# Layer 0 of a two-layer gated cross-attention: value products in pairs, a turned row maximum with full-width weights, and another operation for its rounding

## The reference, cut to what matters

```python
energy = jnp.einsum('nqhd,nkhd->nhqk', q, k)
energy = jnp.where(mask == 0, jnp.float32(-1e+20), energy)
attn = jax.nn.softmax(energy * (1.0 / E ** 0.5), axis=3)
out = jnp.einsum('nhqk,nkhd->nqhd', attn, v).reshape(N, Sq, E)
```

## Time and profile before

| | |
|---|---|
| median of 3 runs | 1371.55 us (1370.35 to 1372.52) |
| the profiled execution | 1371.72 us |
| its span | 1370.0 us |
| PE busy | 1223.5 us, 89% of the span |
| DVE busy | 1026.2 us, 75% |
| ACT busy | 769.0 us, 56% |
| POOL busy | 395.0 us, 29% |
| mean granted TensorE clock | 0.972 |

### The profile page before, as it was taken

How to read it: one execution, slowest core, us unless ns; L and a number is a source line. 1 busy time by engine, 2 the same in 40 slices (tenths; PEclk the granted TensorE clock), 3 DMA queues, 4 the chain that set the end, 5 groups by cost and what they waited for, 6 DMA issues and landing times.

```text
span 1370.0 us, 27816 instructions
## 1 busy us (share of the span) xinstructions
PE 1223.5 (89%) x10408; PEld 760.9 (56%) x10408; DVE 1026.2 (75%) x1662; ACT 769.0 (56%) x1013; POOL 395.0 (29%) x248
## 2 busy tenths in 40 slices
PE   0869899999999996788799999999999999999974
PEld 0335565566566566334356666656666666666642
DVE  6656666666666646877888888888888888888877
ACT  0525455555555555455666666666666666666642
POOL 6357666666566415332000000000000000000000
PEclk9979999999999997999999999999999999999996
DMA  5223244234333420010011110011110011110000
GB/s 151 76 78 79 80 114 113 77 101 110 96 90 104 116 58 18 0 46 0 8 38 46 46 44 22 25 45 45 45 45 20 26 44 45 45 45 23 1 0 14
DMA packets 29717, 74.66 MB, mean 54 GB/s; under 512 B 6384, under 2 KB 14960, under 8 KB 29664
## 3 DMA queue, kind: packets, MB, share of 16 engines
q1 hardware_dynamic: 23408, 70.78, 17.7%
q10 hardware_dynamic: 6256, 3.16, 0.9%
HBM read 42.30 MB, written 0.46 MB: 31 GB/s over the span
## 4 chain that ended last, share of the span: by engine, by line
PE 69%; DVE 13%; issue 8%; ACT 7%; ACTq 3%; POOL 0%; DVEq 0%
PE bank L826 13%; PE bank L808 13%; PE bank L768 8%; PE bank L684 7%; PE bank L708 5%; PE bank L712 5%; PE bank L725 4%; DVE bank_max L1497 3%; ACTq L416 2%; DVE region L1639 2%; PE bank L849 2%; ACT region L1141 2%; PE bank L797 2%; DVE e_row L1458 2%; PE bank L1053 2%
## 5 line engine op out<-in xcount | busy, mean ns | idle before, releaser
L1458 DVE CUSTOM_DVE_ANT_0 e_row<-bank,region 112x1500 f32<-112x1500 f32 x128 | 220.1, 1720 | 129.4 <-PE bank L684 128.4
L1176 ACT CAST region<-bank 125x768 f16<-125x768 f32 x224 | 178.7, 798 | 206.2 <-PE bank L768 206.2
L1141 ACT ACTIVATE region<-bank 125x896 f32<-125x896 f32 x192 | 176.0, 917 | 210.0 <-PE bank L712 209.9
L808 PE MATMUL bank<-region 128*128 128x500 f16 x1008 | 234.6, 378 | 14.7 <-ACT e_row L1167 13.3
L1516 DVE TENSOR_TENSOR region<-bank,region 125x768 f16<-125x768 f32 x224 | 209.7, 954 | 25.4 <-ACT region L1176 25.4
L1497 DVE TENSOR_REDUCE bank_max<-bank 128x1 f32<-128x500 f32 x336 | 208.8, 671 | 10.6 <-PE bank L808 10.6
L514 POOL TENSOR_TENSOR region<-c_in,region 125x1536 f16<-125x1536 f32 x16 | 49.7, 3108 | 560.8 <-ACT region L1191 560.8
L768 PEld LDWEIGHTS bank<-ident,e_row 128*125 128x125 f32 x1344 | 175.5, 188 | 31.2 <-DVE region L1516 5.5
L768 PE MATMUL bank<-ident,e_row 128*125 128x128 f32 x1344 | 179.5, 273 | 3.3 <-DVE region L1516 2.6
L1167 ACT ACTIVATE e_row<-bank,neg_max 128x1500 f32<-128x1500 f32 x112 | 169.7, 1515 | 20.2 <-DVE neg_max L1501 20.0
L808 PEld LDWEIGHTS bank<-region 128*128 (+1 forms) x1008 | 93.3, 98 | 115.6 <-issue 11.4
(11 more groups left out here) (212 smaller groups left out, 1471.0 us busy)
## 6 DMA issues: line engine op xcount, KB each, us to landing
c_in<-in_ctx SPq DMA_DIRECT2D x32, 750.0 KB
region<-region SPq DMA_DIRECT2D x64, 192.0 KB, 2.7
region<-in_mask_Bx1xSxS_if SPq DMA_DIRECT2D x32, 328.1 KB
region<-region SPq DMA_DIRECT2D x64, 96.0 KB, 2.5
region<-region SPq DMA_DIRECT2D x8, 750.0 KB
g_w<-region SPq DMA_DIRECT2D x8, 750.0 KB
g_w<-in_L_ffn_rt_gate ACTq DMA_DIRECT2D x1, 1024.0 KB, 9.9
u_w<-in_L_ffn_rt_up ACTq DMA_DIRECT2D x1, 1024.0 KB, 17.4
```

Source lines behind the costliest of these rows:

```text
L808: last = pe.matmul(bank[:, k, 0:4 * KP], q1[:, ql, b, 128 * t:128 * (t + 1)], c_t1[par][:, cl, 4 * k:4 * k + 4, 0:KP], start=(ql == 0 and ...
L1141: act.activation(p0[:, 2 * i:2 * i + 2, :], ring0("s", h, i)[0:KP, :, 0:HALF_ROWS], ACT.Exp, scale=SCALE0)\
L1176: act.copy(p_high1[grp][:, UC * u:UC * (u + 1), 128 * at:128 * (at + 1)], pair_chunks(unit_no(1, par, ("turn", t, u)), 128)).then_inc(sem( ...
L1458: dve.tensor_tensor_reduce(out=masked.rearrange("p (a k) -> p a k", a=3), in0=bank[0:R0, 0:3, 0:4 * KP], in1=mask_bias[par][:].rearrange(" ...
```

## The change

Three edits, all in layer 0:

1. PV of slots 0 and 1, of 2 and 3, and of 4 and 5 are issued together, ahead of the ST of the even slot.
2. NEG's matmuls have weights of 128 columns (`negc` repeated by a zero stride), write all 128 partitions and not partition 96 alone; `none_valid` has 112 rows and its matmul 112 rows and 128 columns. DVE still reads partition 96.
3. `negc` and `none_valid` are made with `scalar_tensor_tensor`, whose third operand is an array of constants in SBUF: `unfold` (1/FOLD, set once by DVE) and `ones_f`. One wait on the constants, once, before the loop.

```diff
+        unfold = sb("unfold", [128, 4])
-        none_valid = sb("none_valid", [S, 1], F16)
+        none_valid = sb("none_valid", [R0, 1], F16)
@@ pe_neg0
-                last = pe.matmul(place[96:97, 0, R0 * t:R0 * (t + 1)], negc[:, t:t + 1], ident16[0:R0, 0:R0],
+                last = pe.matmul(place[:, 0, R0 * t:R0 * (t + 1)], negc[:, t:t + 1].broadcast_to((R0, 128)), ident16[0:R0, 0:R0],
                                  start=True, stop=True)
             if h == 0:
-                last = pe.matmul(place[0:KP, 1, 0:S], none_valid[:].broadcast_to((S, KP)), ident16[0:S, 0:S],
+                last = pe.matmul(place[:, 1, 0:S], none_valid[:].broadcast_to((R0, 128)), ident16[0:R0, 0:S],
@@ layer0 on PE
                     for i in range(NP):
-                        if has_before:
+                        if has_before and i % 2 == 0:
                             pe_pv0(pe, *before, i)
+                            pe_pv0(pe, *before, i + 1)
@@ dve_neg0
             if h == 0:
-                dve.tensor_scalar(none_valid[:], neg_max[0:S, 0:1], MASKED, None, ALU.is_ge)
-            dve.tensor_scalar(negc[:], neg_max[0:R0, 4 * h:4 * h + 4], FOLD_MAX * FOLD, 1.0 / FOLD, ALU.min, ALU.mult)\
+                dve.scalar_tensor_tensor(none_valid[:], neg_max[0:R0, 0:1], MASKED, ones_f[0:R0, 0:1], ALU.is_ge, ALU.mult)
+            dve.scalar_tensor_tensor(negc[:], neg_max[0:R0, 4 * h:4 * h + 4], FOLD_MAX * FOLD, unfold[0:R0, :], ALU.min, ALU.mult)\
                 .then_inc(sem("negc0"), 1)
@@ the vector block, ahead of its first instructions and ahead of the first maximum
+            dve.memset(unfold[:], 1.0 / FOLD).then_inc(sem("fold_const"), 1)
+            dve.wait_ge(sem("fold_const"), 3)
```

## The result

The changed kernel takes **1470.14 us**, median of 4 runs (1469.48 to 1470.73), where the one before took 1372.0 in the same call (1370.35 to 1372.52): 1.072 times as long [1.0704, 1.0736]. The forecast was 1480, with 1455 to 1496 for the held case.

The account below looks back on a forecast made before the run. The prediction took chains through DVE, not PE, to bound layer 0's loop. 1371.7 + 110.5 (13 held batch ends x 8.5) - 2.6 = 1479.6, say 1480 us; range 1358 to 1496, likeliest case 1455 to 1496.

Parts of the forecast that it names:

- the held case: Batch ends: POOL's mask holds `negc`, NEG 9.3 us after R3 instead of 3.10, 6.2 more, at 13 ends; chance 0.60.
- PE does not set the pace: Layer 0's loop: DVE's links set the distances, so PE's saving of 28 us does not arrive; opposite rival 1344, chance 0.02.
- NEG's full width, 0.2 us each: NEG in each half: full-width weights leave out a switch, saving 0.2 us (0 to 0.3) of its 0.45.
- h=1, -0.2; h=0, 0; with a projection, +0.35: Change per half in layer 0's loop: -0.2 us in 15 h=1 halves, 0 in 8 h=0, +0.35 in 7 with a projection.
- The last half, -1.0: Layer 0's last half has no R and no NEG, so it keeps its gain: -1.0 us.
- L575 in batch 14, -1.1: L575 holds `negc` for 1.32 us in batch 14; PV5 ahead of R3 frees it 2 us earlier: -1.1 us.
- Together -2.6: Layer 0's loop: the changes per half, the last half and L575 add to -2.6 us, without the mask's hold.
- The mask first, by 0.19 us: Batch ends: with PV5 ahead of R3, POOL's mask starts 2.57 us after R3, 0.19 before DVE's two instructions.
- The clock, 2.3 us: After each held batch end, PE's idling brings the 1.2 GHz clock, costing 2.3 us (0 to 3.4).
- The sign that PEclk would be below 9 in most slices of layer 0: Profile after: PE's granted clock, PEclk, was to read below 9 in most slices of layer 0 if the prediction was right.
- The sum: Whole kernel: 1371.7 + 110.5 (13 batch ends x 8.5) - 2.6 = 1479.6, say 1480 us.
- Rival 1, not held: One-input POOL instructions do not hold the new form; L619's hold goes too, 7.8 us: 1361 us (1358 to 1366), chance 0.28.

Follow-up runs that it names:

- mask-late kernel: The changed kernel with one wait added on POOL: the mask instruction starts only when `negc` of that batch end is made; 1374.71 us, 1.002.
- single columns: `negc` made by `tensor_scalar` one column at a time, three ahead of the last maximum: in the changed kernel 1359.95 us, in the kernel before 1361.59 us.

## Why the prediction was right

Point by point, in its order.

- **PE does not set the pace: shown.** With nothing held, the pairs and full width give 1.6 us (1361.59 to 1359.95). An order that keeps PE at work behind DVE's links gave 20.3, with two visits saved per half; the full 28 us were reached by no run.
- **NEG's full width, 0.2 us each: measured 0.18** (unpaired, 51.99 against 52.69 for four halves).
- **h=1, -0.2; h=0, 0; with a projection, +0.35.** The first is right, the last two were too low. From R0 to R0 the mask-late kernel has 12.44, 13.59 and 14.57 us, the one before 12.655, 13.41 and 13.97: -0.2, +0.2 and +0.6. R0 to SPR is 0.17 longer, as laid out (the wait for ACT is 0.26, at 333.19). From SPR to R2 it is 2.09 us for 1.95, where +0.05 was laid out, and with a projection 2.99 for 2.51, where a value product is 0.39: an SPR that had to wait takes 0.08 to 0.09 more to the next piece, and no term had that. The rest of the miss is R3 to NEG in h=0, put at 0.05 less: it stayed 3.10, because `negc` there is held by the end of L561, 0.27 to 0.28 us (0.23 to 0.25 before), and with a projection R0 still comes 0.30 behind NEG.
- **The last half, -1.0: it gave 0.2.** From its NEG to the 96 value products at the end it is 9.75 us in the mask-late kernel (500.71 to 510.46) and 9.94 before: PE got through sooner and then waited for ACT, 0.24 and 0.47 us.
- **L575 in batch 14, -1.1: as said.** The stretch from there to the next batch's end is 25.80 us in the mask-late kernel and 27.02 before.
- **Together -2.6: by these distances about +1.** 15 x -0.22, 8 x 0.18, 7 x 0.60, -0.2 and -1.2 make +0.9, and the loop's end came 0.6 later. By the whole times it is 3.2 (1374.71 less 1371.49), most of it behind the loop, where the prediction had no term.
- **The mask first, by 0.19 us: measured 0.21** (0.12 and 0.13 at two of the 13 batch ends). This was the difference of sums on which the sign hung, and it held.
- **Held: yes, but 5.10 us and not 6.2 + 0.15.** This is the step that was off in size. NEG came 7.99 us after R3 and not 9.3, 4.94 more than in the mask-late kernel and not 6.2. The prediction took POOL's whole duration, as the earlier trace rows show for the operation of before; the new one is let go 1.20 us before the mask's recorded end, though not before L561's. The run with the old operation, held 6.26, is the case that was priced.
- **The clock, 2.3 us: measured 2.6** (16.21 against 13.61, the same kind of half from one NEG to the next, 302.02 to 315.63 in the mask-late kernel). The sign that PEclk would be below 9 in most slices of layer 0 did not come: it was so in four.
- **The sum.** 13 batch ends cost 1470.14 - 1374.71 = 95.4 us, 7.3 each, and not 110.5: 15.1 less. The other terms are +3.2 and not -2.6: 5.8 more. The forecast of 1480 is 10 us from the result because these two errors cancel in part, which is luck; the held term alone would have missed by 15.
- **Rival 1, not held:** false for the new operation, true for one with a PSUM operand. The hold beside the weight scaling was put at 7.8 us. From the third batch end to the fourth it is 26.04 us without it (131.98 to 158.02, single columns) and 32.56 with it (136.00 to 168.56, mask late): 6.5 us. The fourth batch end is 10.5 us apart, but 4.0 of that was there by the second, in part from a hold of 1.12 us by L561 in the first batch.

The Trainium skill (SBUF — State Buffer, Who interferes with whom) has two SBUF inputs as what makes DVE contend with a GpSimd instruction that reads SBUF. The pair of runs with the third operand in SBUF and in PSUM agrees: 5.10 us and 0.16 beside the same mask. The Trainium skill (SBUF — State Buffer, SBUF: two separate sides) also has the later one wait to the other's end. The 6.26 of the old operation beside the mask agrees, and so do the new one's 0.28 beside L561 and 1.29 beside L576; its 5.10 beside the mask (1.20 before the end) and 4.52 beside the weight scaling (0.44 before it) don't. Why is open. The profile's ends of POOL instructions are rough, but the old operation and the new ended at different places of like masks.

## What to carry to other kernels

Before an edit moves work on one engine, look at what the semaphores behind that work start elsewhere, and how many tenths of a microsecond lie between that start and the chain's next link: here 0.2 us of order cost 95. A tiny DVE instruction on a chain, beside long POOL instructions, was safe here as a `tensor_scalar` of one element per partition or with its second operand in PSUM; not with several columns or two SBUF operands. And a saving on PE is only spendable where PE is not waiting: first cover the links, then shorten the work. Last, a few microseconds in the whole time can come from stages that the change does not touch; compare one stretch of the loop too.

## What the runs showed of the hardware

- A DVE `tensor_scalar` of four or five columns is held to the end of a running one-input POOL instruction (6.26 us, to the end of a mask of 6.52); of one column it is not (128 of 128 at 145 to 158 ns, 115 of them wholly beside a POOL instruction).
- `scalar_tensor_tensor` with two SBUF operands is held even for one column. How long depends on what POOL runs: to the recorded end by L561 (two inputs, 14 of 14 within 0.03 us) and by the copy L576 (1.29 us), but only to 1.20 us before the mask's end, and for 4.52 us by L620, which would have gone on to 4.96. With one operand in PSUM it is not held at all (48 of 48 at 0.16 us or less).
- The stretch at 1.2 GHz behind a stall of PE began while PE was still waiting: at 348.0 of a wait that ended at 349.26, and at 215.8 of one that ended at 218.79. It was 6.8 us long in both, so the longer wait left less of it for work. Waits of 5.64 took 2.3 to 2.6 us from the half behind (six halves without a projection, against 13.61), waits of 6.80 took 1.5 to 2.9: a longer stall was often, not always, cheaper for what follows.
